# A transformer layer on one core: dense products as pairs on two 64-row tiles of TensorE, given out in turns between score pairs

## The reference, cut to what matters

```python
xn = layernorm(x)
Q, K, V = (xn @ W.T + b for W, b in ((Wq, bq), (Wk, bk), (Wv, bv)))   # split into 16 heads
Q, K = rope(Q), rope(K)
weights = softmax(causal(Q @ K.T / 4))
attn = (weights @ V) @ Wo.T + bo
h = square(relu(xn @ W_fc.T))          # 1024 wide
y = h @ W_proj.T
spikes = number of spikes in 5 steps of a threshold neuron driven by y, / 5
out = x + attn + spikes
```

## Time and profile before

| | |
|---|---|
| device time, three runs | 2238.79, 2248.03 (median), 2248.32 us |
| span of the profiled execution | 2243.2 us |
| TensorE matmul busy | 2156.2 us, 96% |
| VectorE, ScalarE busy | 1441.2, 1437.5 us, 64% each |
| GpSimd busy | 1097.5 us, 49% |
| mean granted clock of TensorE | 0.987 |

### The profile page before, as it was taken

How to read it: one execution, slowest core, us unless ns; L and a number is a source line. 1 busy time by engine, 2 the same in 40 slices (tenths; PEclk the granted TensorE clock), 3 DMA queues, 4 the chain that set the end, 5 groups by cost and what they waited for, 6 DMA issues and landing times.

```text
span 2243.2 us, 48570 instructions
## 1 busy us (share of the span) xinstructions
PE 2156.2 (96%) x16276; PEld 1406.2 (63%) x16276; DVE 1441.2 (64%) x2134; ACT 1437.5 (64%) x1673; POOL 1097.5 (49%) x1074
## 2 busy tenths in 40 slices
PE   3799999999999999999999999999999999989995
PEld 2656666666666666666666666666666666656653
DVE  5646566766757676566757667676676757646543
ACT  2376766667576675766667576665757667666663
POOL 4455454554645455453545545455464545535431
PEclk9899999999999999999999999999999999999998
DMA  3352544536345353644536354453634635345433
GB/s 137 110 175 88 157 130 115 182 87 197 101 127 168 97 184 88 173 115 132 174 84 192 101 143 144 113 185 84 188 106 120 181 91 181 92 133 155 109 97 94
DMA packets 169785, 298.89 MB, mean 133 GB/s; under 512 B 25089, under 2 KB 114945, under 8 KB 157185
## 3 DMA queue, kind: packets, MB, share of 16 engines
q1 hardware_dynamic: 169600, 296.10, 45.8%
HBM read 174.89 MB, written 103.28 MB: 124 GB/s over the span
## 4 chain that ended last, share of the span: by engine, by line
PE 83%; DVE 6%; ACT 4%; issue 4%; DMA 1%; POOL 1%; SPq 0%; ACTq 0%; DVEq 0%; POOLq 0%
PE pair L1068 33%; PE pair L1264 20%; PE pair L1228 15%; PE pair L1247 15%; ACT probs L708 2%; DVE count L928 2%; DVE stats L792 1%; ACT xT_hi L673 1%; PE pair L1155 1%; DVE h_sq L913 1%; DVE denom L852 1%; ACT h_sq L699 1%; PE pair L1080 1%; DVE numer L951 1%; POOL rot L599 0%
## 5 line engine op out<-in xcount | busy, mean ns | idle before, releaser
L708 ACT ACTIVATE probs<-pair 128x1024 f32<-128x1024 f32 x1152 | 1117.9, 1026 | 490.3 <-PE pair L1247 482.8
L617 POOL TENSOR_SCALAR_AFFINE_SELECT probs<-probs 128x512 f32<-128x512 f32 x512 | 375.0, 752 | 484.8 <-ACT probs L708 484.8
L609 POOL TENSOR_TENSOR h_lo<-h_sq,h_hi 128x512 fp32r<-128x512 f32 x256 | 383.9, 1500 | 437.4 <-DVE h_hi L915 436.9
L1264 PE MATMUL pair<-probs,v_sb 128*17 128x512 f32 (+3 forms) x6144 | 546.9, 489 | 6.1 <-DVE numer L951 5.2
L1247 PE MATMUL pair<-q_ring,k_ring 64*128 64x512 f32 (+3 forms) x3072 | 440.7, 381 | 16.8 <-ACT probs L708 13.7
L913 DVE TENSOR_TENSOR h_sq<-h_sq 128x512 f32<-128x512 f32 x256 | 201.3, 786 | 352.2 <-ACT h_sq L699 352.2
L1247 PEld LDWEIGHTS pair<-q_ring,k_ring 64*128 64x128 f32 x3072 | 227.3, 185 | 272.6 <-ACT probs L708 172.7
L1264 PEld LDWEIGHTS pair<-probs,v_sb 128*17 128x17 f32 x6144 | 152.3, 97 | 297.7 <-issue 264.1
L928 DVE SCALAR_TENSOR_TENSOR count<-y_sb,count 128x512 bf16<-128x512 f32 x256 | 294.1, 1149 | 6.8
L1228 PE MATMUL pair<-wproj_hi,h_hi 128*128 128x256 f32 x1024 | 293.0, 286 | 1.3 <-POOL h_lo L609 1.3
L1228 PE MATMUL pair<-wproj_lo,h_hi 128*128 128x256 f32 x1024 | 289.6, 283 | 0.0
(11 more groups left out here) (89 smaller groups left out, 2592.4 us busy)
## 6 DMA issues: line engine op xcount, KB each, us to landing
q_ring<-qk_dram SPq DMA_DIRECT2D x384, 128.0 KB
k_ring<-qk_dram SPq DMA_DIRECT2D x384, 128.0 KB
qk_dram<-planes SPq DMA_DIRECT2D x64, 512.0 KB, 2.8
qk_dram<-rot_b SPq DMA_DIRECT2D x64, 512.0 KB, 3.9
xn<-in_x SPq DMA_DIRECT2D x17, 1024.0 KB, 7.0
rs<-in_x SPq DMA_DIRECT2D x64, 256.0 KB, 2.7
acc_dram<-rs SPq DMA_DIRECT2D x64, 256.0 KB, 4.5
attn<-numer SPq DMA_DIRECT2D x256, 64.0 KB, 2.3
```

The costliest lines, as they stand in the source:

```text
L609: pool.tensor_tensor(h_lo[i % HB][:, :], h_sq[i % HB][:, :], h_hi[i % HB][:, :].bitcast(F32), ALU.subtract).then_inc(h_lo_done, 1)
L617: ins = pool.affine_select(view, view, [[0, 4], [1, P]], ALU.is_ge, 0.0, base=0, channel_multiplier=-1)
L708: act.activation(probs[BUFFER[n]][:, 2 * pr:2 * pr + 2, :], pair[m % NSLOT][:, :, :], ACT.Exp, scale=SCALE).then_inc(exp_done, 1)
L1264: ins = pe.matmul(pv_bank[32 * i:32 * i + VW, q0 - g * G:G], v_sb[:, kt, 4 * quad + i, :], probs[BUFFER[n]][:, i, at:at + width(kt, g)], s ...
```

## The change

All dense float32r products (query/key, value, expand, contract) are cut into two halves of 64 rows of the contraction. A product's first half (turn 0) runs on one 64-row tile of the array and its second half (turn 1) on the other, accumulating in the same bank. At any time two products run beside each other, one on each tile and each into its own bank: matmul by matmul one and the other in turn. A turn of an item is 12 matmuls of 256 columns per product: an item is now two 128-wide slices for 256 tokens (`expand_part`, `contract_part`), and `expand` of item i + 2 is paired with `contract` of item i. Value products m are paired with each other, or with the contract of the last two items, which are carried over into the next interval (CARRIED = 2). Query/key pairs are the even and odd half.

A step has five places (PLACES = 5). Score pairs are given out one at a time, at places 0, 1, 3 and 4; runs, norms, transposes and output products stand at place 2; dense turns stand after the score pair of their place, by the tables VALUES_AT, QK_AT and MLP_AT. Turns 2k + 1 and 2k + 2 of the MLP use tiles and banks in the same sense and may follow each other; between turns 2k and 2k + 1 there are score pairs or a run. The first matmul of turn 1 waits on a semaphore that the last of turn 0 raises (v_turn, qk_turn, fc_turn, proj_turn). The dense banks are dealt out anew: two (fc_bank) for expand, value and query/key products, one (proj_bank) for contract, transposes and output products. The norm product moves into a score slot, and the third pair of step 8 waits until it has been read (`shift_used`). The other engines' work follows the new places; on SP the stores of planes and of the output move one step later, behind the ring load of step 5, and the first gather from step 6 to step 8. The number of exponentials, masks, rotations and DMAs stays.

```diff
-V_AT = {0: (0, 1)}
-V_EARLY = {1: (2, 3)}
-T_AT = {1: (0, 1, 2), 2: (3,)}
-QK_AT = {2: ((0, 0), (0, 1)), 3: ((1, 0), (1, 1)), 4: ((2, 0), (2, 1)), 5: ((3, 0), (3, 1))}
-O_AT = {3: 0, 4: 1, 5: 2, 6: 3}
-NORM_AT = 7
...
+PLACES = 5
+VALUES_AT = {(0, 0): (0, 0), (0, 3): (0, 1), (0, 4): (1, 0), (1, 0): (1, 1), (1, 3): (2, 0), (1, 4): (2, 1)}
...
+T_AT = {2: (0, 1, 2), 3: (3,)}
+QK_AT = {(2, 4): (0, 0), (3, 0): (0, 1), (3, 4): (1, 0), (4, 0): (1, 1), (4, 4): (2, 0), (5, 0): (2, 1),
+         (5, 4): (3, 0), (6, 0): (3, 1)}
...
+LOW_QK_AT = {(4, 3): 0, (5, 3): 1, (6, 3): 2, (7, 2): 3}
+O_AT = {4: 0, 5: 1, 6: 2, 7: 3}
+NORM_AT = 8
...
+MLP_AT = {(6, 4): (0,), (7, 1): (1,), (8, 1): (2,), (8, 2): (3, 4), (9, 1): (5, 6), (9, 4): (7, 8), (10, 1): (9,),
+          (10, 4): (10,), (11, 1): (11, 12), (11, 4): (13, 14), (12, 1): (15, 16), (13, 1): (17,), (13, 4): (18,),
+          (14, 1): (19, 20), (14, 4): (21, 22), (15, 1): (23, 24), (16, 1): (25,), (16, 4): (26,),
+          (17, 1): (27, 28), (17, 4): (29,)}
...
@@ SP, interval
-                    if more and n == 4:
-                        store_planes(nb, nd, 0)
-                    if last and n in (4, 5):
-                        store_out(b - 1, d - 1, n - 4)
-                    if more and n == 5:
-                        store_planes(nb, nd, 1)
                     if att and n == 5:
                         load_ring(b, d, 2, b * 2 * NUNIT + 2 * NU)
...
+                    if last and n in (5, 6, 7, 8):
+                        store_out(b - 1, d - 1, n - 5)
+                    if more and n in (5, 6, 7, 8):
+                        store_planes(nb, nd, n - 5)
+                    if att and n == 8:
                         gather(b, 0, last)
...
@@ TensorE
+            def query_key(nb, u, turn, tb):
+
                 g, is_k = u // 2, u % 2
                 cols = slice(g * G, (g + 1) * G)
+                if turn:
+                    pe.wait_ge(qk_turn, nb * 4 + u + 1)
+                elif u == 0:
+                    pe.wait_ge(xT_lo_done, tb * 4 + 3)
+                else:
+                    pe.wait_ge(rot_done, nb * 4 + u)
...
+            def expand_part(i, turn, n):
+
+                g, f, k, term = i // ITEMS_OF_GROUP, 2 * (i % ITEMS_OF_GROUP) + n // 6, n // 3 % KD, n % 3
+                rows, m, a = half_rows(i + turn), slice(f * P, (f + 1) * P), n // 6
+                w, x = ((wfc_hi, xT_hi), (wfc_lo, xT_hi), (wfc_hi, xT_lo))[term]
+                return pe.matmul(fc_bank[i % 2][:, a * T2:(a + 1) * T2], w[rows, k, m], x[rows, k, g * T2:(g + 1) * T2],
+                                 start=turn == 0 and n == 0, stop=turn == 1 and n == PART - 1, skip_group_check=True)
...
+            def expand_and_contract(nb, item, i, j, turn, out, copied, first, final):
+
+                await_expand(nb, item, i, turn, first, final)
+                await_contract(item, j, turn, out, copied)
+                for n in range(PART):
+                    h, y = expand_part(i, turn, n), contract_part(j, turn, n)
+                h.then_inc(fc_ps if turn else fc_turn, 1)
+                y.then_inc(proj_done if turn else proj_turn, 1)
...
+                for at in ((n, place) for n in range(NSTEP) for place in range(PLACES)):
+                    n, place = at
+                    if att and place != 2:
+                        scores(b, 2 * n + place // 3, place % 3, last, more)
...
+                    for t in turns.get(at, ()) if more or final else ():
+                        mlp_turn(b, nb, item, t, last, first, final, again)
```

More of the change, by code:

```diff
@@ new lines, in interval @@
+                    if last and place == 2 and n in O_AT:
+                        finish(b - 1, O_AT[n])
+                    if more and at in LOW_QK_AT:
+                        low_qk(nb, LOW_QK_AT[at])
+                    if more and at == (NORM_AT, 2):
+                        bound(nb, first_norm_bank if first else norm_bank)
+                        if first:
+                            replicate_bias()
+                    for i in expanded.get(at, ()) if more or final else ():
+                        activate_h(item, i)
@@ L1000, in interval @@
-                    for u, eo in QK_AT.get(n, ()) if more else ():
-                        rotate(nb, u, eo, items_before(b, again) if att else None)
-                    if last and n in O_AT:
-                        finish(b - 1, O_AT[n], final_bank if final else o_bank)
-                    if more and n == NORM_AT and not first:
-                        bound(nb, norm_bank)
-                    if (more or final) and n in expand_early:
-                        activate_h(item, expand_early[n])
@@ L1017, in interval @@
-                    if more and not first and n == Y1_AT or final and n == Y_FINAL_AT:
-                        take_y(half_of(b, 1, first, final, again), item + NFC - 1)
-                    if first and n == 12:
+                    if first and at == (12, 4):
                         whole_bias()
@@ L1282, in interval @@
                         run(b - 1, LAST_RUN, last)
[L1283 removed]
+                    if att and place == 2 and n in RUN_AT:
                         run(b, RUN_AT[n], last)
[L1285 to L1290 removed]
@@ L1311, in interval @@
[L1311 to L1317 removed]
+                    if more and at == (NORM_AT, 2):
+                        if att:
+                            pe.wait_ge(exp_done, b * 2 * NUNIT + NORM_PAIR - NSLOT + 1)
+                        norms(nb, first_norm_bank if first else norm_bank)
@@ new lines, in interval @@
+                    for m in T_AT.get(n, ()) if place == 2 and (more or final) else ():
+                        transpose(b, tb, m, att, again)
+                    if last and place == 2 and n in O_AT:
+                        output(b - 1, O_AT[n])
+                    if att and at in values_at:
+                        m, turn = values_at[at]
+                        if carried and m < CARRIED:
+                            values_and_contract(b, m, turn, again)
+                        else:
+                            values_together(b, m, turn, again)
```

590 lines of the change are left out of this document (300 added, 290 removed).

## The result

The changed kernel takes 2513.6 us (median of 4 runs, 2512.75 to 2514.42), the kernel before 2244.84 us beside it (4 runs, 2238.79 to 2248.32): 1.120 times as long, 95% interval 1.118 to 1.123. The forecast was 2430 us, with a range of 2200 to 2520; the time is 6 us inside that range and 4 us above the 2340 to 2510 that the prediction held for its own case. The profiled execution has a span of 2511.0 us, 267.8 us more than before's 2243.2.

A forecast was written before the change was run, and what follows sets the result against it. TensorE, busy 96% of the span, was taken as the bound. Terms summed to +11.6 us per interval, +173 over 15, plus 8 in the first: span 2424, forecast 2430 us, range 2200 to 2520.

The forecast's parts named there:

- its own case: Whole kernel: the forecast's summed terms hold, giving 2340 to 2510 us; chance 0.60.
- Part 1: Dense products as pairs on two 64-row tiles: 63.0 us per interval against 62.2, taken as 0.
- second rival: Faster: one tile's weight loads hide under the other's stream, pairs cost 107 and 213 ns, 2195 us; chance 0.18.
- third: Instruction rate: TensorE's instructions come at 38 ns each, a turn takes 1.84 us, 2700 us; chance 0.05.
- Part 2: Changes between scores and dense work: 36 fall away at 0.19 us each, 6.9 us less per interval.
- Part 3: Score pairs waiting for exponentials: four places with no turn between cost +7.6 us per interval, places with one turn +1.35.
- Part 4: Rotary chain: rot_b's store behind SP's ring loads makes TensorE wait; +6.0 us per interval, bounds 2 and 8.
- The second wait: First MLP turn, gated by rotation 3 behind VectorE's work and a store: 0.7 to 2.5 us more, taken as 2.
- Part 5: Shorter leads per interval: transposes to first query/key turn +0.8 us, MLP low part +1.2, other-direction turns +0.5.
- own-turn wait: Other-direction turn waits for its first turn's last matmul, ending 0.28 us after its start; +0.5 us per interval.
- Part 6: Clock after TensorE's waits: half clock now and then, losing up to 1.7 us, taken as +1.0 per interval.
- exponentials alone: Rival: only ScalarE's exponentials are met, rotary and MLP leads hold; +2.5 us per interval, 2290 us; chance 0.14.

The follow-up runs named there:

- e7: Kernel before, with one score pair moved between MLP expansion and contraction at eight steps per steady interval, adding changes of kind: 2305.83 us, 1.0274 of the kernel before.
- e2: Changed kernel with two lone MLP turns moved by one place, so two of four bare score-pair places get a turn: 2449.4 us.
- e3: Changed kernel with the MLP's turns dealt out so every place between two score pairs from step 8 on has a turn: 2380.89 us.
- e1: Changed kernel with SyncE's second-half ring loads moved from step 5 to step 6, behind the stores of units 0 and 1: 2445.95 us.
- e5: Kernel before, with the 13 second-half ring loads put ahead of the store of unit 0's planes and rot_b: 2338.62 us, 1.0423 of the kernel before.
- e4: Changed kernel with both the ring loads behind the stores of units 0 and 1 and the MLP's turns dealt out: 2305.09 us.
- e11: Changed kernel with the score pair ahead of the rot_b wait computed 17 times, same values, to fill the wait: 2496.21 us.
- e6: As e4, but at steps 10, 13 and 16 the other direction's turn stands right behind the first, with no score pair between: 2318.74 us.
- e10: Changed kernel with the score pair ahead of the rot_b wait computed nine times, same values, to fill the wait: 2498.09 us.
- e8: As e4, with the second-half ring loads one step further on, in step 7 behind the store of unit 2: 2289.85 us.

## Why the prediction came out as it did

Direction, place and mechanism of the main waits were right, and the size was short: the sum was 181 us, the span grew by 267.8. Of the 87 us that were missing, 66 are in the 14 steady intervals and 20 outside them. Term by term, for the steady interval at 1378.38 against the one at 950.3 before, in us, from the spacings of the matmul starts (how a spacing is shared between neighbouring parts is partly a choice, so a few tenths may belong to another row):

| part | predicted | measured |
|---|---|---|
| 1, pairs | 0 | +1.0 |
| 2, changes of kind between scores and dense work | -6.9 | -4.0 |
| 3, bare score pairs, and one turn between | +7.6, +1.35 | +6.8, +1.2 |
| 4, rotary chain | +6.0 | +5.0 |
| 5, xT, h_lo, own turn | +0.8, +1.2, +0.5 | +1.2, +2.2, +0.5 |
| 6, clock | +1.0 | +3.7 |
| sum | +11.6 | +17.6 |

The interval grew by 16.6; the 1 us too many is in waits of before that are gone.

**Part 1** was computed as 0.8 and taken as nothing. A turn's pairs start 0.120 us apart and 512-column ones 0.23, as predicted, and neither the 107 ns of the second rival nor the 152 ns (38 ns for each of four instructions) of the third is there:

```profile
1380.37 0.28 PE L1173 MATMUL pair<-xT_hi,wfc_hi 64*128 64x256 f32 x1
1380.37 0.28 PE L1182 MATMUL pair<-wproj_hi,h_hi 64*128 64x256 f32 x1
1380.49 0.28 PE L1173 MATMUL pair<-xT_hi,wfc_lo 64*128 64x256 f32 x1
```

The estimate that the prediction made from the Trainium skill's page "TensorE: Matmul & The Clock Gate", section Part 2 (1.49 us for a turn of 24 matmuls), has 1.44 us of rows beside it (12 x 0.120), which a single product of 128 rows and 256 columns needed as well.

**Part 2** is the step that failed most, by 2.9 us. Its price was right: e7 gives 0.41 us for a change and back. Two counts were wrong. Steps without dense work have no change, so it was 32, not 36: 6.1 us. And 2.1 us came back, beyond the bounds of the part (-6.1 to -8), mostly because a turn's first pair holds the second up after many score pairs:

```profile
1390.18 0.79 PE L1351 MATMUL pair<-q_ring,k_ring 64*128 64x384 f32 x8
1390.81 0.33 PE L1182 MATMUL pair<-wproj_hi,h_hi 64*128 64x256 f32 x1
1390.98 0.28 PE L1182 MATMUL pair<-wproj_lo,h_hi 64*128 64x256 f32 x1
```

0.17 us stand where 0.12 should. It is so at about half of the 33 turns that follow a score pair, by 0.05 to 0.10 us; elsewhere the second pair follows in 0.12. All nine turns behind a score matmul of 128 columns are among them. That such a short last matmul leaves no room for the next load was not tested, and it doesn't account for the others.

**Part 3** held: 1.05 + 0.68 us at a place, where 1.9 were taken from the earlier trace rows. e2 and e3 removed it by its cause.

**Part 4** held in its mechanism, by e1 and e5, and was 1 us too high. Its bounds held (2 to 8). The second wait that it expects, at the first MLP turn, was not there in the changed kernel; it appeared only when other things were faster (e1, e4, e11).

**Part 5** was low for the MLP waits, 1.02 and 1.13 us instead of 0.6 each, at the places that it names. Only the second is put down to h_lo:

```profile
PE pair L1173 <- ACT h_sq L752: 11.7, 14, 0.9
```

At the first ScalarE's relu ended last, 0.07 us behind the low part (1410.55 and 1410.48), so the two are late together. The own-turn wait was 0.28 us in the prediction and is 0.31 to 0.34 in e6.

**Part 6** is the other step that failed. It took a chance of losing 1.7 us now and then. In fact nearly every interval had two such stretches, one behind the rot_b wait and one behind the bare pairs of steps 7 and 8. It priced the waits one by one and did not ask what runs behind each: nine spacings of 0.19 us too much behind rot_b, twelve of 0.09 in the turn behind the bare pairs, and the rest in the work around them. The 3.7 us are an estimate: the spacings within half-clock stretches have some 55 us more than before from 200 us on, over 15 intervals. Another count of the same spacings gives 46 us, 3.1 an interval, and the 0.33 us per us of e10 gives 3.2 for the 9.7 us that a steady interval has more at half clock than before. All lie in the prediction's bounds (0 to 4).

**Outside the steady part** the sum had 8 us on the first interval and half a steady term at either end, 13.8 and 5.8 us; it was 27.3 and 12.1. In the first interval MLP turns follow each other with no score pair between, and each change of direction there shows 0.3 to 1.0 us in the spacings; the query/key products wait up to 5.3 us for the rotation. e4 and e8 leave most of that (20 and 23 us of the 27), and no run took it apart further.

Of the sums, one doesn't come out: the bounds of parts 2 to 6 add up to 1.6 us per interval at the low end, which is about 2270 us and not 2290. That the time fell inside the range owes something to the width that was given for other cases, since the held case ended at 2510.

The rivals: exponentials alone (2290) had its place wrong, as rot_b's wait is real; the faster one fails by the pairs' spacing; the instruction rate fails by 0.120 us.

## What to carry to other kernels

Before work is moved a step later on the engine that sets the time, follow every queue that it passes: 13 loads of 128 KB ahead of one store of 512 KB cost 93 us in a kernel that was otherwise untouched. Where a slot wait paces two producers, put some other work between every two of their pieces; four pieces in a row cost 1.7 us a place here, and dealing the same turns out evenly took 133 us off. And a new wait on TensorE has two prices, its length and the clock of what follows; the second was 0.33 us for each us at half clock here, as other engines set the pace of part of that time.

## What the runs showed of the hardware that was not expected

- Adding 480 or 960 matmuls that only repeat a result made the kernel 15.5 or 17.4 us faster: TensorE was at half clock for 161 and 114 us instead of 206. Not all of the gain in e11 is shown to be the clock's.
- Two products on two 64-row tiles run at the pace of one 128-row product (0.120 and 0.23 us for 256 and 512 columns), with both tiles' weight loads in it, 48 instructions in 1.44 us, 30 ns each, for turns on end.
- Going from 128-row products to 64-row ones and back costs 0.41 us, and staying in the 64-row kind saves less than that suggests, as about half of the turns still have their second pair 0.05 to 0.10 us late.
- A product on the other tile that adds to the same bank, and waits by semaphore for the last product of the first tile, starts 0.31 to 0.34 us later than one that doesn't wait (0.43 to 0.46 us instead of 0.12, e6).
- Repeating matmuls in a loop can bring a stand of its own: 0.9 to 1.5 us in 12 of 14 steady intervals of e11, early in step 0 and far from the repeated work, cause open.
